# Convolution attention: queries and keys of a batch from one product of 128 rows, moved between partitions by SyncE, in place of two products that fill their rows twice

## The reference, cut to what matters

```python
C, CQ, N = 128, 64, 1024                      # B = 8
q = einsum('oc,bcn->bon', Wq, xf) + bq        # 64 x 1024 for each batch
k = einsum('oc,bcn->bon', Wk, xf) + bk        # 64 x 1024
v = einsum('oc,bcn->bon', Wv, xf) + bv        # 128 x 1024
scores = einsum('bcm,bcn->bmn', q, k)
attn = softmax(scores, axis=1)                # over m, the queries' index
out = einsum('bcn,bmn->bcm', v, attn)
return gamma * out.reshape(B, C, H, W) + x
```

## Time and profile before

| what | value |
|---|---|
| median of the 3 runs | 1449.6 us |
| lowest and highest | 1447.02 and 1452.18 us |
| time of the profiled execution | 1451.21 us |
| its span, first to last instruction | 1449.5 us |
| busy: TensorE, VectorE, ScalarE, GpSimd | 1208.4, 933.8, 542.6, 581.1 us |
| `conv_attention` in the span | about 0 to 227.7 us |

### The profile page before, as it was taken

The page is one execution under the profiler, slowest core; times in us unless marked ns, Lnnn a source line. Parts: engine busy times, 40 slices in busy tenths (PEclk is TensorE's granted clock), DMA queues, the critical chain, the costliest instruction groups (busy, mean ns, idle before and its releaser), DMA issues. The chain is left out here.

```text
span 1449.5 us, 31410 instructions
## 1 busy us (share of the span) xinstructions
PE 1208.4 (83%) x11687; PEld 1042.3 (72%) x11687; DVE 933.8 (64%) x2307; ACT 542.6 (37%) x1254; POOL 581.1 (40%) x645
## 2 busy tenths in 40 slices
PE   7999998887492999999995684848489999999960
PEld 4555557677482999999992454635389999999960
DVE  4777775678751754466545875586539877788862
ACT  3444442245451555555553331423133233323310
POOL 5000002000346677747105650057400675577665
PEclk9999999899555999999997895579559999999985
DMA  8600000000402343434214210011111333333343
GB/s 315 283 0 1 0 1 8 1 1 1 139 27 71 116 128 122 129 106 125 90 61 115 85 43 2 1 40 51 33 30 59 111 122 102 99 114 113 107 133 104
DMA packets 93251, 115.50 MB, mean 80 GB/s; under 512 B 18293, under 2 KB 77552, under 8 KB 93104
## 3 DMA queue, kind: packets, MB, share of 16 engines
q1 hardware_dynamic: 72144, 62.73, 14.1%
q0 software_dynamic: 20960, 50.76, 10.8%
HBM read 53.01 MB, written 60.42 MB: 78 GB/s over the span
## 5 line engine op out<-in xcount | busy, mean ns | idle before, releaser
L1413 POOL DMA_INDIRECT sorted_rows<-s_normed,s_places x128 | 137.1, 1071 | 184.2 <-DVE s_places L1359 142.3
L1490 POOL DMA_INDIRECT sx_fetch<-sorted_results,s_places x128 | 138.5, 1082 | 84.0 <-issue 34.7
L1573 PE MATMUL g_bank<-weights,gx_hT 128*128 x1360 | 165.7, 275 | 0.3 <-ACT gx_hT L1601 0.3
L1490 POOL DMA_INDIRECT gx_fetch<-sorted_results,g_places x128 | 130.9, 1023 | 72.8 <-issue 33.1
L1573 PEld LDWEIGHTS g_bank<-weights,gx_hT 128*128 128x128 f32 x1360 | 158.4, 192 | 0.8 <-issue 0.8
L1413 POOL DMA_INDIRECT sorted_rows<-g_normed,g_places x128 | 131.9, 1030 | 67.6 <-issue 36.0
L1536 PE MATMUL s_bank<-sx_xT_high,sx_w_now 128*128 128x256 f32 (+1 forms) x510 | 151.7, 297 | 1.2 <-DVE sx_hT L1648 0.6
L1538 PE MATMUL s_bank<-sx_xT_high,sx_w_now 128*128 128x256 f32 (+1 forms) x510 | 144.2, 283 | 0.0
L1537 PE MATMUL s_bank<-sx_xT_low,sx_w_now 128*128 128x256 f32 (+1 forms) x510 | 143.9, 282 | 0.0
L1601 ACT ACTIVATE gx_hT<-g_bank,gx_b_now 128x256 f32<-128x256 f32 x340 | 133.0, 482 | 3.0 <-PE g_bank L1573 3.0
L1573 PE MATMUL s_bank<-weights,sx_hT 128*128 (+1 forms) x1020 | 129.6, 276 | 3.3 <-issue 1.8
(11 more groups left out here) (434 smaller groups left out, 2749.3 us busy)
## 6 DMA issues: line engine op xcount, KB each, us to landing
sorted_rows<-zeros POOLq DMA_DIRECT2D x29, 512.0 KB, 15.6
gx_xq<-sorted_rows SPq DMA_DIRECT2D x85, 128.0 KB, 2.1
sorted_results<-gx_yq SPq DMA_DIRECT2D x85, 128.0 KB, 2.0
sx_xq<-sorted_rows SPq DMA_DIRECT2D x85, 128.0 KB, 2.1
sorted_results<-sx_yq SPq DMA_DIRECT2D x85, 128.0 KB
feats<-in_x SPq DMA_DIRECT2D x8, 512.0 KB, 7.7
out<-tokens SPq DMA_DIRECT2D x16, 256.0 KB, 3.9
g_raw_up<-in_L_ffn_W SPq DMA_DIRECT2D x1, 2048.0 KB, 9.4
```

The costliest lines, as they stand in the source:

```text
L1413: pool.indirect_dma_start(out=sorted_rows[g], out_offset=bass.IndirectOffsetOnAxis(ap=places[:, at, r:r + 1], axis=0), in_=normed[:, at, : ...
L1490: pool.indirect_dma_start(out=fetch[n % 2][:, i, r, :], out_offset=None, in_=self.sorted_results[g], in_offset=bass.IndirectOffsetOnAxis(a ...
L1573: done = pe.matmul(down[u % 2][:, P * k:P * k + C], hT[u % 2][0:width, i, P * k:P * k + P], self.w_down[0:width, bass.ds(e, 1), i, :].rear ...
```

## The change

For batches 1 to 7, queries and keys come from one product. A fourth block of weights in `packed` holds `Wq` in columns 0 to 63 and `Wk` in columns 64 to 127, with a bias column `bqk` to match. A batch then has four items (two of the joint product, two of values) and not six. ScalarE writes the high parts of both into `q_high` (queries in rows 0 to 63, keys in rows 64 to 127) and VectorE the low parts into `q_low`. SyncE then moves rows: the keys' high part from `q_high` rows 64 to 127 to `k` rows 0 to 63, their low part from `q_low` rows 64 to 127 to `k` rows 64 to 127, and, when both have landed, the queries' two parts from rows 0 to 63 to rows 64 to 127 of `q_high` and `q_low`. The first scores of a batch wait for the last of these four transfers (`doubled`). Batch 0 is done as before. The four items stand in the steps n = 1, 2, 4, 6 (`PLACES`), and are taken one step later.

```diff
-        packed = t.sbuf("conv_packed", [P, 4 * C + 3])
-        wT = [packed[:, P * i:P * i + P] for i in range(3)]
+        packed = t.sbuf("conv_packed", [P, 5 * C + 4])
+        wT = [packed[:, P * i:P * i + P] for i in range(4)]
...
+        PLACES = (1, 2, 4, 6)
+        def items_of(b):
+            return 6 if b == 0 else 4
+        def pairs_of(b):
+            return items_of(b) - 2
+        def given_until(b, items):
+            return sum(items_of(i) for i in range(b)) + items
+        def taken_until(b, items):
+            return sum(pairs_of(i) for i in range(b)) + items
...
+            low, high = slice(0, CQ), slice(CQ, P)
+            for b in range(1, B):
+                sp.wait_ge(qk_ready, taken_until(b, 2))
+                sp.dma_start(k[b % 2][low, :].bitcast(F32), q_high[b % 2][high, :].bitcast(F32)).then_inc(moved, 16)
+                sp.dma_start(k[b % 2][high, :].bitcast(F32), q_low[b % 2][high, :].bitcast(F32)).then_inc(moved, 16)
+                sp.wait_ge(moved, 32 * b)
+                sp.dma_start(q_high[b % 2][high, :].bitcast(F32), q_high[b % 2][low, :].bitcast(F32)).then_inc(doubled, 16)
+                sp.dma_start(q_low[b % 2][high, :].bitcast(F32), q_low[b % 2][low, :].bitcast(F32)).then_inc(doubled, 16)
+            sp.wait_ge(doubled, 32 * (B - 1))
...
-                if item < 4:
-                    w = wT[item // 2]
+                if item < pairs_of(b):
+                    w = wT[item // 2 if b == 0 else 3]
...
-                    pe.wait_ge(qk_ready, b * 4 + 4)
+                    pe.wait_ge(qk_ready, taken_until(b, pairs_of(b)))
+                    if b > 0:
+                        pe.wait_ge(doubled, 32 * b)
...
-                    if 1 <= n <= 6 and b + 1 < B:
-                        project(b + 1, n - 1)
+                    if n in PLACES and b + 1 < B:
+                        project(b + 1, PLACES.index(n))
...
-                if item < 2:
+                if b > 0:
+                    high, low, rows, bias = q_high[b % 2], q_low[b % 2], slice(0, P), bqk
+                elif item < 2:
                     high, low, rows, bias = q_high[b % 2], q_low[b % 2], slice(0, P), bq
...
-                if 2 <= n <= 7 and b + 1 < B:
-                    take_item(b + 1, n - 2)
+                if n - 1 in PLACES and b + 1 < B:
+                    take_item(b + 1, PLACES.index(n - 1))
...
-                if 2 <= n <= 5 and b + 1 < B:
-                    take_projection(b + 1, n - 2)
+                if n - 1 in PLACES[:2] and b + 1 < B:
+                    take_projection(b + 1, PLACES.index(n - 1))
```

More of the change, by code:

```diff
@@ L133, in conv_attention @@
         t = ClearedTools(nc, ctx)
-        packed = t.sbuf("conv_packed", [P, 4 * C + 3])
-        wT = [packed[:, P * i:P * i + P] for i in range(3)]
-        bv = packed[:, 3 * C:4 * C]
-        bq, bk, gamma = (packed[:, 4 * C + i:4 * C + i + 1] for i in range(3))
+        packed = t.sbuf("conv_packed", [P, 5 * C + 4])
+        wT = [packed[:, P * i:P * i + P] for i in range(4)]
+        bv = packed[:, 4 * C:5 * C]
+        bq, bk, bqk, gamma = (packed[:, 5 * C + i:5 * C + i + 1] for i in range(4))
         q_high = [t.sbuf(f"q_high{i}", [P, N], F32R) for i in range(2)]
@@ L156, in conv_attention @@
         qk_ready = t.sem("qk_ready")
+        moved = t.sem("k_moved")
+        doubled = t.sem("q_doubled")
         v_taken = t.sem("v_taken")
@@ L204, in project @@
                 else:
-                    pe.wait_ge(qk_ready, b * 4 + item - 1)
+                    pe.wait_ge(qk_ready, taken_until(b, item - 1))
                 bank = proj[item % 2]
-                if item < 4:
-                    w = wT[item // 2]
+                if item < pairs_of(b):
+                    w = wT[item // 2 if b == 0 else 3]
                     pe.matmul(bank[:, :], w[:, :], feats[:, b, HALF * (item % 2):HALF * (item % 2) + HALF],
@@ L212, in project @@
                     for j in range(4):
-                        at = P * (4 * (item - 4) + j)
+                        at = P * (4 * (item - pairs_of(b)) + j)
                         done = pe.matmul(bank[:, P * j:P * j + P], feats[:, b, at:at + P], wT[2][:, :],
@@ L262, in take_low @@
             def take_low(b, item):
[L263 removed]
+                dve.wait_ge(qk_high, taken_until(b, item + 1))
                 at = slice(HALF * (item % 2), HALF * (item % 2) + HALF)
[L265 removed]
+                if b > 0:
+                    high, low, rows, bias = q_high[b % 2], q_low[b % 2], slice(0, P), bqk
+                elif item < 2:
                     high, low, rows, bias = q_high[b % 2], q_low[b % 2], slice(0, P), bq
@@ L273, in take_item @@
             def take_item(b, item):
-                if item < 4:
+                if item < pairs_of(b):
                     take_low(b, item)
                 else:
-                    take_values(b, item - 4)
+                    take_values(b, item - pairs_of(b))
             def row_max(s):
@@ L328, in take_projection @@
             def take_projection(b, item):
-                into, bias = ((q_high, bq), (k, bk))[item // 2]
+                into, bias = ((q_high, bq), (k, bk))[item // 2] if b == 0 else (q_high, bqk)
                 at = slice(HALF * (item % 2), HALF * (item % 2) + HALF)
-                act.wait_ge(proj_ready, b * 6 + item + 1)
+                act.wait_ge(proj_ready, given_until(b, item + 1))
                 act.activation(into[b % 2][:, at], proj[item % 2][:, :], ACT.Identity,
@@ L2657, in laid_out @@
     arrays["conv_packed"] = np.concatenate(
-        [q.T, q.T, k.T, k.T, v.T, np.broadcast_to(given["L0_conv_bv"], (P, C)),
+        [q.T, q.T, k.T, k.T, v.T, q.T, k.T, np.broadcast_to(given["L0_conv_bv"], (P, C)),
          column(np.tile(given["L0_conv_bq"], 2)), column(np.tile(given["L0_conv_bk"], 2)),
+         column(np.concatenate([given["L0_conv_bq"], given["L0_conv_bk"]])),
          np.broadcast_to(given["L0_conv_gamma"], (P, 1))], axis=1)
```

2 lines of the change are left out of this document (1 added, 1 removed).

## The result

| what | before | after |
|---|---|---|
| median of 20 runs each | 1446.7 us | 1452.0 us |
| lowest and highest | 1440.8 and 1452.2 | 1446.7 and 1456.4 |
| span of the profiled execution | 1449.5 us | 1451.1 us |
| `conv_attention`, first scores to SyncE's first transfer of the next stage | 210.9 us | 212.0 us |
| from there to SyncE's first transfer after the linear attention | 133.0 us | 135.0 us |

The change made the kernel slower, by a ratio of 1.0035 (95% interval 1.0021 to 1.0049), 5.3 us by the medians. The forecast was 1440.1 us, with a range of 1436.3 to 1447.0. The three runs that were known before had a median 2.9 us above that of the 20 runs.

What follows compares the result with a forecast made beforehand. TensorE's own instruction list was taken to bound the convolution attention. Terms of -12.0 (products), +0.2 (weights) and +2.3 us (moves beside fills) summed to -9.5, giving 1440.1 us, range 1436.3 to 1447.

Steps and rivals of the forecast that it cites:

- What bounds the kernel: Convolution attention: TensorE's instruction list sets the pace; 14 fewer products at 0.855 us each save 12.0 us.
- VectorE and ScalarE: Convolution attention steps: both engines stay off TensorE's path despite thinner steps, with 1.7 us of slack; costed at nothing.
- The weights: Load before the first matmul: packed grows from 515 to 644 columns, 66 KB, costing +0.2 us on the path.
- The moves, undisturbed: SyncE's transfers per batch: a pair takes 4.4 us, two 8.8, under 11.2 us of cover, so +0.
- Rival B: Moves too slow in every batch: 6.3 us a pair, net 1450.6, no change; decides at 5.6 us; chance 0.10.
- The moves beside the fills: Batches 1 and 2, moves meeting GpSimd's zero fills: TensorE waits 2.0 and 0.3 us, +2.3, bounds 0 and 6.
- the equal-shares case: Batch 1's moves and the fills split the DMA engines equally: pair 5.7 us, two 11.4, wait 0.2.
- Rival C: Batch 1's moves queue behind all fills issued before: TensorE waits +22 us, net 1460, slower; chance 0.07.
- Everything behind the stage "only shifts": Stages after the convolution attention start behind a barrier of all engines and only shift in time.
- The chances: Whole kernel: faster, below 1445.3 us, 0.79; same 0.12; slower 0.09, from C and the worse part of B.

Runs made afterwards that it cites:

- e2: Changed kernel with the 34 zero fills moved from the convolution attention to the linear attention: 1439.8 us, ratio 0.9953 to the kernel before.
- e5: Kernel before with the packed operand as wide as the changed kernel's, the added columns unused: 1444.6 us, ratio 0.9992 to the kernel before.
- e3: Changed kernel with batches 1 and 2 done as before, joint product and moves only from batch 3: 1442.4 us, ratio 0.9970 to the kernel before.
- e4: Changed kernel with at most two zero fills under way: 1438.7 us, ratio 0.9943 to the kernel before.
- e6: Changed kernel with two fills under way and narrow packed weights, GpSimd joining them on chip: 1440.9 us, ratio 0.9962 to the kernel before.
- e8: Changed kernel with two fills under way and two more unread TensorE products in the last batch: 1437.5 us, ratio 0.9947 to the kernel before.
- e11: Changed kernel, fills unpaced, three moves per batch issued at once, ScalarE and VectorE writing 64 rows per instruction: 1439.9 us, ratio 0.9954 to the kernel before.

## Why the prediction was wrong, point by point

**What bounds the kernel.** Right. In this stage TensorE's own list sets the pace, and an item costs 0.855 us: e2's stage is 11.9 us shorter where the sum said 12.0.

**VectorE and ScalarE.** Right: no wait of TensorE for either, beyond the one of the earlier trace rows.

**The weights.** +0.2 was taken. The first product starts at 6.62 us in the profile after and 6.48 in the one before, but over all profiles it starts between 6.04 and 6.48 us with the narrow operand and between 6.12 and 6.62 with the wide one. The term is too small to be seen here, and e5 puts its price within the noise.

**The moves, undisturbed.** A pair was put at 4.4 us between bounds of 3.1 and 5.0, and takes 4.2. The choice between the bounds had no row behind it, so that it came this close is partly luck; that the pair stays under 5.6 is not. Two take 8.4 of the 11.2 us of cover, and in batches 3 to 7 nobody waits. Rival B falls: its half-rate data is what the trace shows, its fixed part of 3.8 us is 1.6 to 1.8.

**The moves beside the fills: the step that failed.** The prediction took 2.3 us "bounds 0 and 6"; the wait was 10.3. The sum allowed a pair 5.7 us with equal shares, and at most 8.0 with half-rate data under sharing and "some time for what is already in the engines". The sharing, once it began, was within that: the rest of a pair after its first packet took 5.8 to 6.1 us. What failed is the other part of the term. For "what is already in the engines" the upper bound has about 1 us left (8.0, less 1.8 fixed and some 5 for data of half rate under sharing), the equal-shares case nothing, and the forecast lay between the two; it measured 4.2 us for the first pair and 3.2 for the second, beyond the 1.0 us that any move's first packet takes. It came twice, because the second pair waits for the first. In numbers: 1.0 + 3.2 undisturbed, 4.2 of delay and 2.6 of sharing are the first pair's 11.0; the two together are 21.3 where the cover is 11.2. Rival C had this mechanism, a move behind fills that were issued before it, but with the whole queue of 18 us ahead, and was given 0.07. The truth lay between the forecast and C: some fills are ahead of a move, up to about 2 MB of them. The prediction named two prices for one question, "almost none" and "all", and the row that spoke for the middle was there: a fill took up to 28.0 us to land, so far more had been handed over than the engines could work on, and nothing in the trace said how much of it they had already taken in.

The Trainium skill's rule (each DMA engine goes round between its queues, packet by packet, "DMA: Bandwidth & Descriptors", section "Queues, rings and completion order") was read as speaking for equal shares from the start. The trace agrees with it only from 5 us after the issue on: from 33.0 to 35.5 us the moves (q1) have 93 packets and the fills 97.

```profile
q1 hardware_dynamic: 93, 0.32, 58.2%
q0 software_dynamic: 97, 0.40, 43.1%
```

The delay before that is the measurement's, and it is what the term lacked.

**The clock.** No term of the sum had it. A wait of 10 us for TensorE cost 2.6 us more in the steps behind it in one profile and 1.3 in the other, at 1.2 GHz. The prediction priced long waits at their length alone.

**Everything behind the stage "only shifts".** Wrong by 4 to 6 us in the medians of the changed kernel, e2, e3, e4 and e6, by 2 in e8 and by nothing in e11. About 2 us of the change's own show in its first profile, in the linear attention (135.0 against 133.0), and 0.9 in its second (133.9).

**The chances.** Slower had 0.09, nearly all of it on a single wait of over 12 us. Wait, clock and later stages together come to some 17, with no single part of that size. Against the forecast of -9.5 the measured +5.3 is 14.8 us more: 8.0 from the wait, 1.3 to 2.6 from the clock behind it, and the rest from behind the stage, of which only a part has a cause here.

## What to carry to other kernels

Before a short transfer that someone waits for is issued while another queue has large transfers under way, count not only the sharing, but what the DMA engines have already taken in: here 3 to 4 us more for each dependent round trip, and about 3 us more for the sharing. Three cures were measured. Letting GpSimd have only two fills under way cost nothing and turned a loss of 5 us into a gain of 7.7; four were not enough. One round trip in place of two gained 7.4, and moving the fills to a later stage 6.7; the runs do not tell the three apart. Where TensorE stands idle for some us, add what the low clock costs after it; and where a stage's length changes by a few us, expect the next stage to differ by 1 to 2 us for reasons of its own, and judge the stage by its own stretch of the trace, in more than one profile.

## What the runs showed of the hardware

- A SyncE transfer that was issued beside a long queue of GpSimd's large fills moved its first packet 5.2 us later (4.2 for the pair after it), against 1.0 with no fills about. 2.0 MB of fills went through in between, with eight of 512 KB under way 1.8 MB. With four it was 2.5 us and 1.0 MB, with two 2.0 us and 0.8 MB.
- A pair of 256 KB landed after 4.2 us undisturbed, after 5.7 to 6.8 with two fills under way (three profiles), and after 10.8 to 11.5 with four, eight or no limit.
- An SBUF to SBUF transfer of 64 rows with 4 KB each ran at about 210 GB/s, against 413 for fills from 128 rows.
- With full queues SyncE's second issue of a pair took 1.3 to 1.6 us at batch 1, where it takes 0.6 with empty ones; the first took 0.5 to 0.6 with either. SyncE had nothing else to do.
- After pauses of about the same length (5.2 to 5.7 us at the seam) the clock was at half for 3.4 to 6.9 us, also within one kernel, and the stretch behind was up to 3 us longer with more of it.
